# Second attention: values of all heads in one bank, division after the weighting, jobs that run over batch borders, and a third of the turned probabilities copied by VectorE

## The reference, cut

```python
# _L1_attn_ref, per batch b: 16 heads of 8 channels, 256 tokens
q, k, v = heads_split(x @ Wq), heads_split(x @ Wk), heads_split(x @ Wv)
q, k = q * cos + rotate_half(q) * sin, k * cos + rotate_half(k) * sin
scores = q @ k.T / sqrt(8) + bias[h]          # bias by distance, from rel_emb
attn = softmax(where(causal, scores, -1e9))
out = (attn @ v).reshape(b, s, d) @ Wo
```

## Time and profile before

| | us |
|---|---|
| median of the runs shown | 2417.43 |
| the profiled execution | 2419.39, its span 2417.5 |
| PE busy in the span | 2280.3 (94%) |
| DVE, ACT, POOL busy | 1755.6 (73%), 1379.3 (57%), 1596.8 (66%) |
| third stage: first scores to last weighting | 1814.5 to 2122.0 |
| mean granted PE clock | 0.974 of full speed |

### The profile page before, as it was taken

The page is one execution under the profiler, slowest core; times in us unless marked ns, Lnnn a source line. Parts: engine busy times, 40 slices in busy tenths (PEclk is TensorE's granted clock), DMA queues, the critical chain, the costliest instruction groups (busy, mean ns, idle before and its releaser), DMA issues.

```text
span 2417.5 us, 81630 instructions
## 1 busy us (share of the span) xinstructions
PE 2280.3 (94%) x34944; PEld 1563.9 (65%) x34944; DVE 1755.6 (73%) x2707; ACT 1379.3 (57%) x2778; POOL 1596.8 (66%) x931
## 2 busy tenths in 40 slices
PE   7789999999999999999999999999968888889998
PEld 5456666666666666666666666666646666656665
DVE  3678887888788878887888788878838888822322
ACT  2256666666666666666666666666626666633332
POOL 1298888898889888988898889888912322101111
PEclk9899999999999999999999999999979999989999
DMA  4011112111221112111221112211130000000000
GB/s 115 3 38 36 33 35 66 44 34 33 57 53 34 34 31 70 42 34 32 54 58 34 31 36 60 52 32 35 35 113 1 1 1 1 1 1 5 5 5 5
DMA packets 77303, 83.91 MB, mean 35 GB/s; under 512 B 24964, under 2 KB 48786, under 8 KB 76946
## 3 DMA queue, kind: packets, MB, share of 16 engines
q1 hardware_dynamic: 76946, 78.70, 12.7%
HBM read 26.56 MB, written 1.07 MB: 11 GB/s over the span
## 4 chain that ended last, share of the span: by engine, by line
PE 62%; DVE 20%; issue 10%; ACT 5%; POOL 3%; SPq 0%; ACTq 0%; DMA 0%; POOLq 0%; DVEq 0%
PE bank L564 8%; PE bank L645 7%; PE bank L657 6%; DVE n L1266 5%; PE lnbank L585 4%; PE obank L634 4%; ACT qk L941 3%; PE bank L575 3%; PE obank L626 3%; PE sbank L601 3%; PE bank L665 3%; PE bank L856 3%; PE obank L611 3%; PE obank L866 2%; PE sbank L866 2%
## 5 line engine op out<-in xcount | busy, mean ns | idle before, releaser
L1259 DVE TENSOR_TENSOR qk<-bank,tab 128x1024 f32<-128x1024 f32 x384 | 468.7, 1221 | 194.7 <-ACT qk L941 194.6
L1577 POOL TENSOR_TENSOR rn<-n2m,cst 128x16 f32<-128x16 f32 x192 | 562.8, 2931 | 16.0
L1573 POOL TENSOR_TENSOR qk<-qk 128x1024 f32<-128x1024 f32 x192 | 454.6, 2368 | 156.9 <-DVE qk L1259 156.9
L564 PE MATMUL bank<-wqk,xs 128*128 128x512 f32 x768 | 405.0, 609 | 1.7 <-DVE qk L1259 0.9
L941 ACT ACTIVATE qk<-bank 128x512 f32<-128x512 f32 x384 | 226.9, 591 | 314.0 <-PE bank L564 314.0
L1581 POOL TENSOR_TENSOR qk<-qk,rn 128x1024 f32<-128x1024 f32 x192 | 365.4, 1903 | 28.1 <-POOL rn L1577 0.9
L575 PEld LDWEIGHTS bank<-cst,qk 128*128 128x128 f32 x1536 | 191.5, 141 | 215.3 <-issue 170.7
L575 PE MATMUL bank<-cst,qk 128*128 128x128 f32 x1536 | 231.8, 274 | 11.0 <-POOL qk L1581 11.0
L1266 DVE TENSOR_REDUCE n<-qk 128x16 f32<-128x1024 f32 x192 | 232.1, 1209 | 0.0
L1585 POOL TENSOR_TENSOR lnr<-lnv,cst 128x2 f32<-128x2 f32 (+1 forms) x76 | 54.3, 714 | 244.1 <-DVE lnv L1143 244.1
L585 PE MATMUL lnbank<-wv,xs 128*64 128x512 f32 x768 | 208.0, 620 | 0.0
(11 more groups left out here) (357 smaller groups left out, 4231.0 us busy)
## 6 DMA issues: line engine op xcount, KB each, us to landing
vp<-vp SPq DMA_DIRECT2D x672, 65.0 KB, 2.0
wqk<-in_L_ffn_Wqkv SPq DMA_DIRECT2D x24, 256.0 KB, 3.6
wv<-in_L_ffn_Wqkv SPq DMA_DIRECT2D x6, 512.0 KB, 3.9
wo<-in_L_ffn_Wo SPq DMA_DIRECT2D x6, 512.0 KB, 4.2
xs<-Z SPq DMA_DIRECT2D x48, 64.0 KB, 2.4
xs<-Z SPq DMA_DIRECT2D x48, 63.8 KB, 2.1
vp<-in_L_ffn_w SPq DMA_DIRECT2D x1, 2048.0 KB, 13.7
mw<-in_L_ffn_w SPq DMA_DIRECT2D x8, 256.0 KB, 6.8
```

Source lines behind the costliest of these rows:

```text
L564: nc.tensor.matmul(bank[s % 2][:, :], xs[:, odd, WIN + r * P:WIN + r * P + P], wqk[:, lo:lo + 512], start=True, stop=True).then_inc(p_full, 1)
L1259: tt(qk[:, both, :].rearrange("p o (h d) -> p o h d", d=DH), heads(bank[c % 2][:, :]).unsqueeze(1).broadcast_to([P, 2, PAIRS, DH]), table. ...
L1573: tt(direct, direct, swapped, ALU.add).then_inc(sum_done, 1)
L1577: tt(rn[:, m % 2, :], n2m[:, :], const("mhalf"), ALU.pow).then_inc(rn_done, 1)
```

## The change

- `JOBS` goes by y = 0 to 3: job 3y has r = 0 and heads y, y + 4, y + 8, y + 12; jobs 3y + 1 and 3y + 2 have r = 1 and heads (y, y + 4) and (y + 8, y + 12).
- Scores of one y are issued together (`scores3`), eight matmuls into the four banks `quad`, each contracting over 32 rows only. POOL masks the queries over 4 heads instead of 16 (`qm` is 2 x 4 x 256 wide, two buffers).
- Bias and maximum are one DVE instruction per head, `tensor_tensor_reduce`: 32 in a batch.
- The probabilities aren't normalised. The values are placed, by a shifted window into a zero-padded tile, such that the four heads of 32 rows accumulate in the same rows, and all 16 heads fill one bank. ACT copies that bank (`take_raw`), DVE inverts the 32 sums of the batch and spreads them (`invert`), PE turns them into the same bank (`spread_inverses`), DVE multiplies (`divide3`). `out3` is one matmul.
- `px`, `sh` and `mx` have three buffers. A batch has 12 slots; the jobs of the next follow at once. Jobs with r = 0 have their turned probabilities copied by DVE, the others by ACT. ACT's slot has the exponentials first and then the copy of job n - 2.
- The bias table moves to a tile of its own and is loaded once after the first layer of stage 2; the expert weights `mw2` move to `kT` and `tab`. `Wo` is one load, and a memset of `wv` is gone.

The new functions and loops, PE's first, then ACT's, then DVE's:

```diff
+            def scores3(b, odd, y):
+                if y == 0:
+                    pe.wait_ge(s3["qk"], 2 * b + 2)
+                    pe.wait_ge(s3["qm"], b + 1)
+                wait(pe, s3["mx"], NJ * b + 3 * y)
+                for r in range(2):
+                    w = P * (r + 1)
+                    for g in range(4):
+                        rows = slice(WIN * g, WIN * g + WIN)
+                        mm = nc.tensor.matmul(quad[:, g, P * r:P * r + w], qm[rows, odd, y, r * P:r * P + P],
+                                              s3k[odd][rows, 0:w], start=True, stop=True)
+                mm.then_inc(s3["full"], 1)
...
             def step3(b, odd, next_batch, batch_before):
                 u = 3 * b + (LN_S3 + 1)
-                for m in range(NJ + 3):
-                    attend(b, odd, m)
+                for m in range(NJ if next_batch else NJ + 4):
+                    n = NJ * b + m
+                    if 2 <= n <= NJ * B + 1:
+                        turn3(n - 2)
+                    if m in (2, 5, 8):
+                        scores3(b, odd, m // 3 + 1)
+                    if m == NJ - 1 and next_batch:
+                        scores3(b + 1, 1 - odd, 0)
+                    if 3 <= n <= NJ * B + 2:
+                        weigh3(n - 3)
                     if next_batch:
                         prepare(b + 1, m, u if batch_before else LN_S3 + 2)
                     if batch_before:
+                        finish(b - 1, m, u + 2 if next_batch else u)
+                    if m == 3 and batch_before:
+                        spread_inverses(b - 1)
...
+            def exps3(b, m):
+                n = NJ * b + m
+                r, heads = JOBS[m]
+                w = P * (r + 1)
+                act.wait_ge(s3["mx"], n + 1)
...
+                    if m < NJ:
+                        exps3(b, m)
+                    if 2 <= n <= NJ * B + 1 and n % 3 != 2:
+                        take_turned3(n - 2)
...
+            def shift3(b, m):
+
+                n = NJ * b + m
+                r, heads = JOBS[m]
+                w = P * (r + 1)
+                dve.wait_ge(s3["full"], 4 * b + m // 3 + 1)
+                wait(dve, s3["px"], n - 2)
+                for x, h in enumerate(heads):
+                    last = nc.vector.tensor_tensor_reduce(out=s3sh[n % 3][:, x * w:x * w + w], in0=quad[:, h // 4, P * r:P * r + w],
+                                                          in1=bias[:, h, S - w:S], scale=-1.0, scalar=3e38, op0=ALU.add,
+                                                          op1=ALU.min, accum_out=mx[:, n % 3, x:x + 1])
+                last.then_inc(s3["mx"], 1)
...
+                    if m < NJ:
+                        shift3(b, m)
+                    if 2 <= n <= NJ * B + 1 and n % 3 == 2:
+                        take_turned3(n - 2)
+                    if m == 2 and batch_before:
+                        invert(b - 1)
                     if next_batch:
                         prepare(b + 1, 1 - odd, m, u if batch_before else LN_S3 + 2)
                     if batch_before:
                         finish(b - 1, m, u + 2 if next_batch else u)
+                    if m == 3 and batch_before:
+                        divide3(b - 1)
```

More of the change, by code:

```diff
@@ L64, in unit1 @@
     return LN_S1 + UNITS1.index((j, n))
-JOBS = [job for n in range(0, H, 4)
-        for job in ((0, range(n, n + 4)), (1, range(n, n + 2)), (1, range(n + 2, n + 4)))]
+JOBS = [job for y in range(4)
+        for job in ((0, range(y, H, 4)), (1, range(y, H // 2, 4)), (1, range(H // 2 + y, H, 4)))]
 NJ = len(JOBS)
@@ L744, in out3 @@
             def out3(b):
[L745 to L748 removed]
+                pe.wait_ge(s3["ot"], b + 1)
+                nc.tensor.matmul(lnbank[:, S:2 * S], s3wo, s3ot, start=True, stop=True).then_inc(s3["y"], 1)
             def prepare(b, slot, u):
@@ new lines, in turn3, with placed, weigh3 @@
+            def turn3(n):
+                pe.wait_ge(s3["px"], n + 1)
+                wait(pe, s3["pts"], n)
+                for q in range(4):
+                    mm = nc.tensor.transpose(bank[2][:, q * P:q * P + P], s3px[n % 3][:, q * P:q * P + P], ident)
+                mm.then_inc(s3["ptf"], 1)
+            def placed(odd, kb, h):
+                lo = WIN * h + WIN - HD - HD * (h % 4)
+                return vs[:, odd, kb, :, :].rearrange("p h n -> p (h n)")[:, lo:lo + WIN]
+            def weigh3(n):
+                b, m = n // NJ, n % NJ
+                r, heads = JOBS[m]
+                y = m // 3
+                pe.wait_ge(s3["pts"], n + 1)
+                if m == 0:
+                    pe.wait_ge(s3["v"], b + 1)
+                    wait(pe, s3["ot"], b - 1)
+                lo = r * P
+                for kb in range(r + 1):
+                    for x, h in enumerate(heads):
+                        row, q = WIN * (h // 4), x * (r + 1) + kb
+                        mm = nc.tensor.matmul(bank[b % 2][row:row + WIN, lo:lo + P], placed(b % 2, kb, h),
+                                              pT[:, n % 2, q * P:q * P + P], start=(m == 0), stop=(y == 3 and kb == r),
+                                              skip_group_check=True)
+                mm.then_inc(s3["pv"], 1)
@@ L834, in _ @@
             step3(B - 1, 1, False, True)
-            for slot in range(9, 13):
-                finish(B - 1, slot, LN_S4 - 1, False)
+            for slot in range(8, 12):
+                finish(B - 1, slot, LN_S4 - 1)
             pe.wait_ge(ld_gate, 64)
```

251 lines of the change are left out of this document (107 added, 144 removed).

## The result

The changed kernel takes 2403.95 us (2396.76 to 2407.84, four runs) beside 2418.11 for the kernel before on the same chip: ratio 0.9937, 95% interval 0.9911 to 0.9964, faster by 0.6%. The forecast was 2430, slower. The time lies inside the range, 2398 to 2470, but the direction was wrong.

What follows compares the result with a forecast made beforehand. DVE's list bounds the third stage now, PE close behind; after the change a chain of waits does, 38.9 us a batch against 38.7. 2419.4 - 3 + 16 (clock) = 2432, 2.0 above the median, so 2430; range 2398 to 2470.

Steps and rivals of the forecast that it cites:

- The chain: Third stage: waits between PE, DVE and ACT set the time, 38.9 us a batch against 38.7; likeliest case, chance 0.42.
- five steps: One round: PE transposes, weighting, step; DVE step, fused pair; PE scores; DVE step, four fused; ACT four exponentials, then copy.
- the ring: The closed round of waits PE, DVE, PE, DVE, ACT, back to PE's transposes; four rounds a batch.
- 4.45: Fixed us per round: transposes and weighting 1.2, weighting 0.6, exponentials 1.55, copy 0.6, hand-overs 0.5.
- hand-overs: Delays between engines in a round: 0.15 us behind PE, 0.05 behind the others, 0.5 in total.
- The sums: Each engine's work per batch after the change: DVE near 22 us, ACT 21.6, PE near 24.
- a = 0.34 and b = 0.48: Forecast us per fused DVE instruction of 128 and 256 columns; 16 of each, 13.1 us a batch.
- The rival with cheap instructions: Fused 0.31 and 0.445, s = 0.8, clock holds: -12 chain, -10 clock, 2408 (2396 to 2416); chance 0.26.
- The score tiles: PE's four row tiles run side by side, s = 1.0 us per score group; in series 3.0.
- The third rival: The maximum is an instruction of its own: a = 0.465, b = 0.60, batch 41.3 us, time 2450; chance 0.14.
- The clock: PE idles about 3 us a round, so its clock falls more often: 2 us a batch, +16 in all.
- step 5: ACT's four exponentials, 1.55 us, then the 0.58 copy that PE's next transposes wait for.

Runs made afterwards that it cites:

- e2: Changed kernel with ACT copying the turned probabilities of two jobs back before a job's exponentials, not after: 2352.77 us, ratio to the kernel before 0.9731.
- e3: Changed kernel with DVE copying in slots with n mod 3 = 0 instead of n mod 3 = 2, ACT in the others: 2374.16 us.
- e6: Changed kernel with DVE's fused instructions one slot earlier, ahead of the slot's norm or projection step: 2352.3 us, ratio to the kernel before 0.973.
- e4: Changed kernel with all copies of turned probabilities on ACT, none on DVE: 2404.41 us.
- e7: Changed kernel with the reorderings of e2 and e6 together, DVE copying in slots with n mod 3 = 1: 2309.36 us, ratio to the kernel before 0.955.
- e9: Changed kernel with extra unused fused instructions, two per narrow job and one per wide job, to reach about the forecast price: 2439.21 us, ratio to before 1.0089.
- e11: Changed kernel with the bias table's load put back behind the last waits of stage 2: 2404.05 us.
- e1: Changed kernel with one addition and one maximum per job in place of the fused instructions: 2449.22 us, ratio to the kernel before 1.0135.
- e14: Kernel before with only ACT's copy moved behind the exponentials: 2454.92 us, ratio 1.0152.
- e15: Kernel before with the fused instructions and ACT's copy moved behind the exponentials: 2420.22 us, ratio 1.0005.
- e12: Kernel before with only its addition and maximum per job replaced by the fused instruction per head: 2388.18 us, ratio 0.9882.
- e13: The e9 kernel plus five unused matmuls ahead of PE's round-opening transposes in three of four rounds: 2421.18 us.
- e5: Changed kernel plus five unused matmuls ahead of PE's round-opening transposes in three of four rounds: 2395.21 us, ratio to the kernel before 0.9905.

## Why the prediction was right or wrong

- **The chain, right.** That the engines' savings become idle time, and by which five steps, is what the waits show. e2, e3 and e6 move the time by taking a step out, e4 not at all by moving what is in no step. With the ring broken the same work takes 2309 (e7). The round shown above is one with variance, broadcast and addition: with the measured prices the prediction's terms for it, 4.45 + 0.87 + 2 x 0.345 + 4 x 0.21 + 1.9, make 8.75, and it took 8.72. (Its hand-overs are the wrong way round: PE starts 0.15 behind the others, as at 1923.04 behind the copy's end at 1922.89, and the others 0.03 behind PE, as DVE's step at 1916.08 behind PE's end at 1916.05. The total of 0.5 is near.)
- **The sums, nearly.** DVE 18.4 (forecast near 22; the fused instructions, 8.9 in place of 13.1, account for it), ACT 20.7 (21.6), PE 23.1 at full clock in e7 (24). With the smaller masks DVE's additions beside them fell as forecast, from 0.91 and 1.36 to 0.42 and 0.43.
- **The step that failed: the price of the fused instruction**, in "With 0.03 between instructions these are 0.31 and 0.445" and the premium put on top, a = 0.34 and b = 0.48. Measured: 0.21 and 0.345, below the floor. The 0.03 was read from pairs in which the second waits for the first; the fused ones don't wait for each other. The kernel before has such pairs too, in DVE's timeline, and they were not used:

```profile
1963.57 0.69 DVE L1419 TENSOR_REDUCE mx<-sh 128x2 f32<-128x512 f32 x1
...
1964.37 0.69 DVE L1428 TENSOR_TENSOR px<-px,rdn 128x512 f32<-128x512 f32 x1
1964.98 0.41 DVE L1139 TENSOR_TENSOR lnd<-aoT,lnbank 128x256 f32<-128x256 f32 x1
```

  The multiplication is recorded 0.69 long, and the next instruction, which doesn't depend on it, begins 0.61 after its start. With 0.61 for 512 columns, 0.08 less than its record, a plain instruction of 128 would have been put at 0.20. At the forecast price the kernel is in fact slower than before (e9), so this step also turned the direction.
- **In the sum.** With a = 0.21, b = 0.345 and s = 0.87 a batch is 17.8 + 3.5 + 2.8 + 2.5 + 9.15 = 35.7 in place of 38.9. That is 3.2 x 8 = 25 us: 2430 - 25 = 2405, measured 2404.
- **The rival with cheap instructions, near by luck.** Its bound, 8b + 12a + 4s below 11, was met at 8.8, and its 2408 lies 4 us from the time. But it got there by -12 for the chain and -10 for a clock that holds; the chain gave -25 and the clock did not hold (0.89). Its price too, 0.31 and 0.445, was a floor that the instructions went below.
- **The score tiles, right.** s = 1.0 forecast, 0.87 measured (scores at 1917.12, the next PE instruction at 1917.99): the row tiles run side by side. No gap for a change of tiling shows: the weighting at 1917.99 begins before the scores' recorded end at 1918.06, and in e7, where scores follow transposes without a wait, they begin at 1912.72, before the transposes' recorded end at 1912.79.
- **The third rival, half right.** The maximum is a second instruction, but at price 0. The Trainium skill, VectorE: DVE Perf Modes, section Two Vector instructions with no wait between them, says that an operation with an accumulator output is two instructions, and the trace agrees (CUSTOM_DVE_ANT_0 and DVE_READ_ACCUMULATOR2_ANT); the price that the rival put on it is what the trace does not show.
- **The clock, right in kind, too constant in size.** Forecast: 2 us a batch. What is left over the chain's sum in the changed kernel is 37.3 - 35.7 = 1.6 in its fastest execution and 2.4 in e11 (38.1). But in e9, near the forecast's own chain with 35.7 + 2.6 = 38.3, a batch is 42.6: 4.3. At the forecast price the kernel takes 2439 and not 2430, so the clock's term, too small there, kept the forecast 9 us nearer to the time than its price alone would have: that is luck. The idle stretches of a round were forecast at about 3 us; shown here are 1.38 and 2.63. PE's idle time in a batch is 9.7 us with the clock at 0.89, 11.3 at 0.80 in e9 and 12.3 at 0.77 in e1, but 5.8 both in e2 at 0.92 and in e6 at 1.00, so the total alone doesn't settle the clock. In one place PE is idle for 1.37 us, then come transposes at full speed, then these stretches and the same eight scores in 1.59 in place of 0.87:

```profile
1895.41 0.63 PE L791 MATMUL bank<-cst,ao 128*128 128x128 f32 x4 [1.37 <-ACT pT L1080]
...
1898.20 1.67 PE L782 MATMUL quad<-qk 32*128 32x128 f32 x16
1899.79 0.91 PE L813 MATMUL bank<-pT,qT 128*32 128x128 f32 x8
```
```profile
1896.50:1898.50 2.00, 1.96 (x14) 1.55 (x16) 1.09 (x6) 0.92 (x3) 0.69 (x1) 0.62 0.00 0
1898.50:1900.00 1.50, 1.50 (x18) 0.83 (x16) 0.50 (x1) 0.71 (x4) 0.00 (x0) 0.50 0.00 0
```

- **A side claim, wrong.** "The chain is there today too, but DVE's load covers it." For step 5 it isn't covered: the kernel before has ACT's copy ahead of the exponentials, and turned round it loses 37 us (e14). The prediction described step 5 rightly but didn't price it against the order of before, so it never said that this one part of the change costs some 32 to 51 us (e15 against e12, the change against e2).
- **A reading of the kernel before, wrong.** DVE's waits for scores, 4.6 us a batch, don't lie at the border, and inside a batch DVE does stop. In the batch around they are 1.26 at the border, but 1.77 at job 10, behind `out3` in PE's list (1.99), and 0.81 and 0.32 at jobs 2 and 5:

```profile
1962.84 0.69 DVE L1416 TENSOR_TENSOR sh<-sbank,tab 128x512 f32<-128x512 f32 x1 [1.77 <-PE sbank L790]
...
1972.10 0.69 DVE L1416 TENSOR_TENSOR sh<-sbank,kT 128x512 f32<-128x512 f32 x1 [1.26 <-PE sbank L790]
```

  The border costs DVE 1.3 us a batch, not some 5. The sum didn't use this term, but it fits e14: DVE's load was no closed cover.
- **Around the stage.** Early bias load at 0: right (e11). The single `Wo` load was not tested by itself. The first scores come 1.2 us earlier than before in e11 and 3.7 in the changed kernel's profile; 1.5 was forecast.

## What to carry to other kernels

Price instructions from start to start, and read that from pairs that stand to each other as yours will: on DVE here a pair with a wait between them cost the record and 0.03, a pair without cost 0.07 to 0.08 less than the record. When a change empties an engine, write down the ring of waits before adding up sums, then look for two neighbours in a list of which the one that waits longest stands ahead of the one that others wait for; here swapping such a pair was worth 51 us, over three times the whole change. Idle time of PE isn't free when its clock falls with it: expect the clock to cost more the longer the ring leaves PE idle, and don't carry one constant from a short ring to a longer one.

## What the runs showed of the hardware

- DVE overlaps neighbours without a wait between them, plain additions and multiplications as well as fused ones: 0.28 recorded, 0.20 to 0.21 from start to start for 128 columns; 0.42 and 0.345 for 256; 0.69 and 0.61 for 512. The Trainium skill, VectorE: DVE Perf Modes, section The DRAIN you can't avoid, says of the flush after an operation that it can't be skipped "by chaining ops without semaphores", and in the same section that a next one which isn't held starts earlier; these rows agree with the second.
- The read of the accumulator on DVE, 0.08, costs nothing between fused instructions; ACT's, 0.18 to 0.20, begins 0.09 before the exponential's recorded end, and the next exponential of 128 columns begins 0.38 to 0.40 after the last. Behind a copy, which has no such read, the next ACT instruction begins 0.09 before the record ends (0.56 and 0.47), so the read adds some 0.09.
- Five unused matmuls in PE's idle stretch, in three of four rounds, made the kernel faster by 18 us in e13, with the clock at 0.89 in place of 0.80; in e5, where the clock had fallen less, by 9 us in the medians.
